# Mamba scan states kept one column apart: the product with C shifted by a column, the last states copied by ScalarE in fours

## The reference, cut to what matters

```python
def step(h, inp):                       # 4 sequences of 1024 positions
    x_t, dt_t, B_t, C_t = inp
    dA = jnp.exp(dt_t[..., None] * A)
    h = dA * h + (dt_t * x_t)[..., None] * B_t[:, :, None, :]
    y = jnp.einsum('bgpn,bgn->bgp', h, C_t)
    return (h, y)
...
y = y + x.reshape(b, l, D_INNER) * D_param
y = y * jax.nn.silu(z)
return y @ out_proj_w.T
...
h = hidden_states + _mamba(_rmsnorm(hidden_states, norm1_w), ...)
xn = _rmsnorm(h, norm2_w)
mlp = jax.nn.silu(xn @ gate_w.T) * (xn @ up_w.T) @ down_w.T
return h + mlp
```

## Time and profile before

| | us |
|---|---|
| median of 3 runs | 1143.21 (1143.1 to 1143.37) |
| the profiled execution | 1142.64 |
| its span, first to last instruction | 1140.6 |
| PE busy | 1027.5 (90%) |
| DVE busy | 1009.3 (88%) |
| POOL busy | 931.2 (82%) |
| ACT busy | 627.9 (55%) |

### The profile page before, as it was taken

The page is one execution under the profiler, slowest core; times in us unless marked ns, Lnnn a source line. Parts: engine busy times, 40 slices in busy tenths (PEclk is TensorE's granted clock), DMA queues, the critical chain, the costliest instruction groups (busy, mean ns, idle before and its releaser), DMA issues.

```text
span 1140.6 us, 13548 instructions
## 1 busy us (share of the span) xinstructions
PE 1027.5 (90%) x3844; PEld 537.2 (47%) x3844; DVE 1009.3 (88%) x1133; ACT 627.9 (55%) x1235; POOL 931.2 (82%) x540
## 2 busy tenths in 40 slices
PE   3566689999999999999999999999999989899998
PEld 1222134546454554546453554546453543446777
DVE  4689899999999999999999999999999989997342
ACT  4464675548655675548655675548655554443320
POOL 2689899888999899888999899888999989886100
PEclk9696689999999999999999999999999989899999
DMA  6999899998979798998989798988979797860000
GB/s 230 227 209 196 187 237 245 234 194 187 230 180 218 166 232 192 210 198 189 227 186 214 166 239 185 216 196 189 232 176 204 165 229 163 175 148 19 0 1 18
DMA packets 120121, 208.41 MB, mean 183 GB/s; under 512 B 16816, under 2 KB 25968, under 8 KB 119920
## 3 DMA queue, kind: packets, MB, share of 16 engines
q1 hardware_dynamic: 118320, 203.85, 79.8%
q0 software_dynamic: 1008, 3.67, 0.9%
q10 hardware_dynamic: 720, 0.04, 0.0%
HBM read 178.65 MB, written 12.06 MB: 167 GB/s over the span
## 4 chain that ended last, share of the span: by engine, by line
PE 59%; POOL 15%; issue 8%; ACT 8%; DVE 7%; DMA 1%; SPq 1%; DVEq 0%; POOLq 0%; ACTq 0%
PE p_r L560 17%; PE p_r L549 11%; POOL h_s L1352 9%; PE p_y L515 7%; PE p_r L555 6%; PE p_dt L504 5%; DVE h_s L1083 4%; POOL bt_s L1322 3%; PE p_r L566 2%; PE p_dt L660 2%; PE p_r L660 2%; ACT p_dt L716 2%; PE p_r L535 2%; ACT tok L765 2%; PE p_r L670 1%
## 5 line engine op out<-in xcount | busy, mean ns | idle before, releaser
L1352 POOL TENSOR_TENSOR h_s<-h_s,c_s 128x1024 f32<-128x1024 f32 x255 | 601.9, 2365 | 69.9 <-DVE h_s L1083 52.2
L716 ACT ACTIVATE p_dt<-p_dt,an_s 128x512 f32<-128x512 f32 x400 | 260.7, 660 | 274.2 <-PE p_dt L504 273.9
L1083 DVE TENSOR_TENSOR_SCAN h_s<-p_dt,carry,bt_s 128x512 f32<-128x512 f32 x256 | 319.4, 1271 | 7.8 <-ACT p_dt L716 7.2
L1083 DVE TENSOR_TENSOR_SCAN h_s<-p_dt,bt_s 128x512 f32<-128x512 f32 x256 | 303.2, 1211 | 15.5 <-ACT p_dt L716 13.3
L504 PE MATMUL p_dt<-kdt,pick_s 128*128 128x512 f32 x400 | 253.5, 647 | 56.3 <-DVE h_s L1083 44.2
L1322 POOL TENSOR_TENSOR bt_s<-bt_s,b_s 128x1024 f32<-128x1024 f32 x101 | 239.0, 2366 | 12.3 <-DMA bt_s<-dx_rows 7.5
L560 PE MATMUL p_r<-nT,w_s 128*128 128x512 f32 x448 | 208.3, 601 | 0.3
L1066 DVE TENSOR_TENSOR bt_s<-bt_s,p_b 128x1024 f32<-128x1024 f32 x155 | 186.3, 1202 | 8.8 <-DMA bt_s<-dx_rows 8.8
L504 PEld LDWEIGHTS p_dt<-kdt,pick_s 128*128 128x128 f32 x400 | 78.6, 200 | 193.8 <-DVE h_s L1083 104.1
L515 PE MATMUL p_y<-h_s,ysel_s 128*32 128x512 f32 x1024 | 143.1, 633 | 14.8 <-POOL h_s L1352 14.5
L549 PE MATMUL p_r<-nT,gu_s 128*128 128x512 f32 x308 | 144.6, 599 | 5.9 <-ACT nT L916 5.9
(11 more groups left out here) (153 smaller groups left out, 955.4 us busy)
## 6 DMA issues: line engine op xcount, KB each, us to landing
bt_s<-dx_rows SPq DMA_DIRECT2D x512, 256.0 KB, 5.7
dtr_s<-dt_rows SPq DMA_DIRECT2D x224, 128.0 KB, 6.5
kdt<-st_dt SPq DMA_DIRECT2D x64, 128.0 KB, 5.4
tok<-in_x SPq DMA_DIRECT2D x8, 512.0 KB, 8.5
xo<-in_x SPq DMA_DIRECT2D x8, 512.0 KB, 3.8
xr_s<-xb_s SPq DMA_DIRECT2D x64, 64.0 KB, 5.5
b_s<-xb_s SPq DMA_DIRECT2D x64, 64.0 KB, 5.2
dx_rows<-dx_s SPq DMA_DIRECT2D x16, 256.0 KB, 6.5
```

The costliest lines, as they stand in the source:

```text
L716: A(p_dt[DT_BANK[u]][:, :], dt_in, ACT.Exp, scale=an_s[:, c:c + 1]).then_inc(a_dA, 1)
L1083: V.tensor_tensor_scan(h_s[:, u % 8, :], p_dt[DT_BANK[u]][:, :], bt_s[:, u % 16, :], carry[:, u:u + 1] if par else 0.0, ALU.mult, ALU.add) ...
L1352: G.tensor_tensor(h_s[:, two, :], h_s[:, two, :], c_s[:, h, :].unsqueeze(1).broadcast_to([P, 2, T]), ALU.mult)\
```

## The change

The slots of `h_s` get 513 columns. The scan writes columns 1 to 512, the product with C reads columns 1 to 512 and writes columns 0 to 511, and TensorE sums columns 0 to 511. So column 512, the last state, is not overwritten by the product, and the product waits for nobody's copy. ScalarE copies column 512 of four units at once in all even tiles, in slot 4m + 6 for units 4m to 4m + 3; the last group of a tile is copied in slot 2 of the next one. GpSimd copies nothing any more. VectorE's scan of unit 4m + 8 waits for the copy of group m after an even tile's unit has used the slot, since it overwrites the column.

```diff
+CAR_LAG = 6
...
-        h_s = sb("h_s", [P, 8, T])
+        h_s = sb("h_s", [P, 8, T + 1])
...
-                                            h_s[:, u % 8, :], start=(m % 8 == 0), stop=(m % 8 == 7))
+                                            h_s[:, u % 8, 0:T], start=(m % 8 == 0), stop=(m % 8 == 7))
...
-            def keep_carry(k):
-
-                act.wait_ge(v_sc, 2 * k + 2)
-                two = slice(2 * k % 8, 2 * k % 8 + 2)
-                A(carry[:, 2 * k:2 * k + 2], h_s[:, two, T - 1], ACT.Copy).then_inc(a_car, 1)
+            def keep_carry(i, m):
+
+                act.wait_ge(v_sc, i * U + 4 * m + 4)
+                four = slice(4 * m % 8, 4 * m % 8 + 4)
+                A(carry[:, 4 * m:4 * m + 4], h_s[:, four, T], ACT.Copy).then_inc(a_car, 1)
...
-                    if known(i) and i == 0 and u % 2 == 0 and u >= 2:
-                        keep_carry(u // 2 - 1)
+                    if units and i % 2 == 0 and u >= CAR_LAG and (u - CAR_LAG) % 4 == 0:
+                        keep_carry(i, (u - CAR_LAG) // 4)
+                    if i >= 1 and i % 2 and u < CAR_LAG and (u - CAR_LAG) % 4 == 0:
+                        keep_carry(i - 1, (u + U - CAR_LAG) // 4)
...
-                    if known(i) and i == 0 and u == U - 1:
-                        keep_carry(PAIRS - 1)
...
-                    if par and known(i) and i == 1:
-                        dve.wait_ge(a_car, k + 1)
-                    elif par:
-                        dve.wait_ge(g_car, (i - 3) * (PAIRS // 2) + k + 1)
+                    if par:
+                        dve.wait_ge(a_car, i // 2 * 16 + u // 4 + 1)
+                if u % 4 == 0 and n >= 8 and (n - 8) // U % 2 == 0:
+                    t, group = (n - 8) // U, (n - 8) % U // 4
+                    dve.wait_ge(a_car, t // 2 * 16 + group + 1)
...
-                V.tensor_tensor_scan(h_s[:, u % 8, :], p_dt[DT_BANK[u]][:, :], bt_s[:, u % 16, :],
+                V.tensor_tensor_scan(h_s[:, u % 8, 1:T + 1], p_dt[DT_BANK[u]][:, :], bt_s[:, u % 16, :],
...
-                        if known(i) and i == 0:
-                            pool.wait_ge(a_car, k + 1)
-                        elif par == 0:
-
-                            G.tensor_tensor(carry[:, u - 1:u + 1], h_s[:, two, T - 1], one_s[:, :], ALU.mult)\
-                                .then_inc(g_car, 1)
-                            pool.wait_ge(g_car, (i - 2) * (PAIRS // 2) + k + 1)
...
-                            G.tensor_tensor(h_s[:, two, :], h_s[:, two, :],
+                            G.tensor_tensor(h_s[:, two, 0:T], h_s[:, two, 1:T + 1],
                                             c_s[:, h, :].unsqueeze(1).broadcast_to([P, 2, T]), ALU.mult)\
                                 .then_inc(g_hc, 1)
```

More of the change, by code:

```diff
@@ L245, in build @@
         v_fa, v_hd, v_o = sem("v_fa"), sem("v_hd"), sem("v_o")
-        g_rr, g_rr2, g_car, g_bt, a_car = (sem(n) for n in ("g_rr", "g_rr2", "g_car", "g_bt", "a_car"))
+        g_rr, g_rr2, g_bt, a_car = (sem(n) for n in ("g_rr", "g_rr2", "g_bt", "a_car"))
         g_hc, g_r, g_r2, g_r3, g_dx, g_hx = (sem(f"g_{n}") for n in ("hc", "r", "r2", "r3", "dx", "hx"))
@@ L1334, in body @@
                         pool.wait_ge(v_sc, i * U + u + 1)
-                        G.tensor_tensor(h_s[:, u % 8, :], h_s[:, u % 8, :], c_s[:, 1, :], ALU.mult).then_inc(t_h62, 1)
+                        G.tensor_tensor(h_s[:, u % 8, 0:T], h_s[:, u % 8, 1:T + 1], c_s[:, 1, :], ALU.mult)\
+                            .then_inc(t_h62, 1)
                     if units and u % 2:
@@ L1341, in body @@
                             pool.wait_ge(a_c[h], i + 1)
-                        if known(i) and i == 0:
-                            pool.wait_ge(a_car, k + 1)
-                        elif par == 0:
-                            G.tensor_tensor(carry[:, u - 1:u + 1], h_s[:, two, T - 1], one_s[:, :], ALU.mult)\
-                                .then_inc(g_car, 1)
-                            pool.wait_ge(g_car, (i - 2) * (PAIRS // 2) + k + 1)
                         if i == LAST and u == U - 1:
-                            G.tensor_tensor(h_s[:, u % 8, :], h_s[:, u % 8, :], c_s[:, h, :], ALU.mult).then_inc(g_hc, 1)
+                            G.tensor_tensor(h_s[:, u % 8, 0:T], h_s[:, u % 8, 1:T + 1], c_s[:, h, :], ALU.mult)\
+                                .then_inc(g_hc, 1)
                         else:
-                            G.tensor_tensor(h_s[:, two, :], h_s[:, two, :],
+                            G.tensor_tensor(h_s[:, two, 0:T], h_s[:, two, 1:T + 1],
                                             c_s[:, h, :].unsqueeze(1).broadcast_to([P, 2, T]), ALU.mult)\
```

## The result

The changed kernel took 1134.25 us (median of 11 runs, 1132.13 to 1141.15), the kernel before 1142.98 (11 runs, 1139.82 to 1143.37). The ratio is 0.9931, with a 95% interval of 0.9919 to 0.9944: faster by 0.7%, 7.9 us (the two medians taken by themselves differ by 8.7). The forecast was 1136.7 with 6.5 us less. The profiled execution after took 1132.13 us, the fastest of its 11, with a span of 1129.9 us. It shows best where time went; how much goes by the medians.

A forecast was written before the change was run, and what follows sets the result against it. Three nearly full engines cap tiles from 1 on; in tile 0 GpSimd waits for copies. Gains 3.7 + 3.3 less 0.5 make 6.5 us: 1142.64 to 1136.1, plus 0.57 for the median, 1136.7 us; range 1132.0 to 1141.6.

The forecast's parts named there:

- What bounds: From tile 1 TensorE, VectorE and GpSimd are nearly full; relieving one brings at most the others' 4 to 6 us idle.
- The wait in tile 0: GpSimd's product no longer waits for ScalarE's copy of the last states: 3.7 us gain, ends 1.8 and 4.5.
- The waits for sums: Tile 0 after 87 us: VectorE's 1.8 us idle for TensorE's sums, which wait for products, goes.
- The decays: Tile 0 after 87 us: VectorE's 2.7 us idle for decays goes, except 0.8 left of the longest, 1.9.
- GpSimd's copies: Removing GpSimd's 96 copies in tiles 2, 4 and 6: 3.3 us gain, half of the upper end 6.6.
- The step named: Start of even tiles: four copies fewer ahead of GpSimd's power, tokens 0.7 us earlier, TensorE's 1.3 us wait shrinks.
- The odd tiles' half of the term: Change from even to odd tile: GpSimd 1.1 us earlier, TensorE's waits for tokens and `nT` shrink, up to 1.5 us.
- ScalarE's copies: 64 four-unit copies added on ScalarE, 32 of two units removed: 0.5 us loss, between none and 4.8.
- VectorE's new wait: Scan 4m + 8 waits for group m's copy, which stands ahead of a decay it awaits anyway: costs nothing.
- The shifted operands: GpSimd's product with C on shifted columns: no term in the sum, product expected to stay at 2365 ns.
- the dearer product: Third rival: two runs and the shift lengthen all 256 GpSimd products; 1144.7 us at 0.185 us more each. Chance 0.15.
- The signs: If right: no carry wait, product 2365 ns, tile 0 near 108 us, its late VectorE idle about 1, even-tile-start `nT` wait near 0.6.

The follow-up runs named there:

- e5: Changed kernel with rows of 516 columns, read from column 1, so new order without the shorter product (2362 ns): 1134.22 us, ratio 0.9933.
- e6: Changed kernel with rows of 516 columns, read from column 2 and written from column 1, all product rows short (2000 ns): 1132.46 us, ratio 0.9923.
- e7: Kernel before with only C moved two columns later, in rows of 516; all copies and waits kept: 1134.25 us, ratio 0.9922.
- e9: e5 with tile 0's wait back, ScalarE copying pairs and GpSimd waiting for them: 1137.44 us, ratio 0.9962.
- e10: e5 with GpSimd's copies back in tiles 2, 4 and 6, tile 0 as changed: 1137.30 us, ratio 0.9960.
- e3: Kernel before with only the 513-column layout and shifted product, all copies, waits and queues kept: 1133.99 us, ratio 0.9931.

## Why the prediction was right, point by point

**What bounds.** Right. GpSimd was the engine to relieve, and the relief is capped by the two others. The prediction said that no relief can bring a tile more than the others idle for its sake; that agrees with two independent reliefs of 7.9 us that give 7.9 together, and with the equal lengths of tiles 2 to 6 in after, e5, e6 and e7.

**The wait in tile 0, 3.7 us.** e9 against e5 measures 3.2 by the medians, and tile 0 shrank by 3.4. Size right, composition wrong. The waits for sums were put at 1.8 and are worth 3.0: the fourth of them ends at 150.32, just outside the window of the earlier trace rows, and each costs 0.1 to 0.25 us more than its idle time, as a pair of scans takes 2.52 us behind a wait and 2.33 otherwise. The decays were to fall from 2.7 to 0.8 us and fell to 2.6; taking their twin of the earlier trace rows as the price of the longest was the mistake. The two errors nearly cancel, which is luck. Tile 1 gave 2.0 us in the profiled pair that the sum didn't have: VectorE's waits for decays there fell from 2.7 to 1.2 us and the one for a sum (0.5, the fourth above) went. With e9's 1.6 us in tile 1 the wait's price in the traces is 4.8 us, 3.2 of it in tile 0; the term stopped at the end of tile 0.

**GpSimd's copies, 3.3 us.** e10 against e5: 3.1, net of ScalarE's 48 copies. The half that was taken between nothing and 6.6 was the right one, but it rested on no row, and the two medians leave it uncertain by nearly its size. The step named, tokens, `nT`, gate, is there: TensorE's wait for `nT` fell from 1.3 to 0.7 as foretold, and in tile 4 VectorE gains 0.8 us at one place, the scan behind the gate's first product, and nowhere else. The odd tiles' half of the term had the wrong step, and its size is luck. Of 1.5 us it counted up to 0.8 for tokens, but TensorE waits 0.9 for them in tile 5 before and after. Tile 5 is 1.0 shorter all the same: 0.2 lies at scan 27, behind the gate's last tanh and as much as the wait for `nT` fell (0.7 to 0.5), and 0.8 at scans 53 and 56, near its end, where decays came late before. Why these came late was not followed up.

**ScalarE's copies, 0.5 us, and VectorE's new wait, nothing.** No engine waits for any of the 64 copies (mean 0.20 us) in the trace after. Neither was undone alone. That they cost next to nothing is argued, not shown: no wait names them, and the two terms above make 3.2 + 3.1 = 6.3 of the 7.9, known no better than to some 3 us each.

**The shifted operands: zero, "and no gain".** This is the step that failed. The reason given, that as many elements pass, left the gain out of the term's bounds, and the argument for zero from the products with C and B being alike compared two kinds that both had their reads at equal columns. The product is 183 ns shorter, and without any change of the order this alone gives the same median (e3). The forecast held because the two reliefs overlap: from tile 2 on the same cap stops both. That is luck as far as this term goes, for nothing in the prediction had such a relief.

The rule of the Trainium skill that spoke for the dearer product (GPSIMD Engine Reference, Performance pitfalls for Q7 kernels) is a read command of about 102 cycles that does not pipeline with the one before. The runs do not show it for a second run of 512: e5's product, two runs on both sides, takes 2362 ns, and the flat one of before 2365. The Trainium skill's rule on lines of 16 bytes (Advanced Engine Details and Errata, SBUF Cachelines) names the unit within which the runs here do see a difference, but gives no price to where two reads stand in it; here it is some 360 ns in 2365. The dearer product that the prediction estimated from it, 0.02 us for a start at column 1, does not show in e5 (2362 against 2365).

**The signs.** As foretold: no wait for a carry, tile 0 near 108 (108.6), ScalarE's idle before its tokens gone, `nT` near 0.6, tiles 2 to 6 each 0.8 to 1.0 shorter. Missed: the product of 2365, and VectorE's idle time of about 1 us in tile 0 (2.6).
